# Two layers of attention and experts: shared sums by bank, token lists a step later, and an earlier turning of block 1

## The chip, the cores and the metric

The kernel runs on one core of a Trainium2 chip. Its time is the device time of one launch, in microseconds (us). The engines are TensorE (PE in the profile; its weight loads are PEld), VectorE (DVE), ScalarE (ACT), GpSimd (POOL) and SyncE (SP), which only issues transfers here. Each engine runs its own instructions in the order of the program, and waits on semaphores for the others.

## The reference

The input is 8 batches of 512 tokens with 256 channels, 4096 tokens in all. Four sublayers follow one another, each on the layer norm of what came before, each added to it. The change touches the second one, the first expert layer, in its shared part and in its routing.

```python
def _layernorm(x, axis=-1, eps=1e-05):
    m = jnp.mean(x, axis=axis, keepdims=True)
    v = jnp.var(x, axis=axis, keepdims=True)
    return (x - m) / jnp.sqrt(v + eps)

# x: (8, 512, 256), fp32. _L0_attn_ref is an attention without softmax (keys times values, then queries).
def _L0_ffn_ref(x, gate_w, wg, wu, wd, swg, swu, swd):     # 8 experts, top 2, INTER 352, 704 shared
    xf = x.reshape(-1, H)
    logits = xf.astype(jnp.float32) @ gate_w.astype(jnp.float32).T
    scores = jax.nn.softmax(logits, axis=-1)
    topw, topi = jax.lax.top_k(scores, TOP_K)
    denom = topw.sum(axis=-1, keepdims=True) + 1e-20
    topw = topw / denom * SCALE
    wdense = jnp.zeros((T, N_EXPERTS), jnp.float32).at[jnp.arange(T)[:, None], topi].set(topw)
    hg = jnp.einsum('th,ehi->eti', xf, wg)
    hu = jnp.einsum('th,ehi->eti', xf, wu)
    eo = jnp.einsum('eti,eih->eth', jax.nn.silu(hg) * hu, wd)
    y = jnp.einsum('te,eth->th', wdense, eo)
    shared = jax.nn.silu(xf @ swg) * (xf @ swu) @ swd
    return (y + shared).reshape(B, S, H)
...
    x = x + _L0_attn_ref(_layernorm(x, axis=-1), L0_attn_wq, L0_attn_wk, L0_attn_wv, L0_attn_wo)
    x = x + _L0_ffn_ref(_layernorm(x, axis=-1), L0_ffn_gate_w, L0_ffn_wg, L0_ffn_wu, L0_ffn_wd, L0_ffn_swg, L0_ffn_swu, L0_ffn_swd)
    x = x + _L1_attn_ref(_layernorm(x, axis=-1), ...)   # windowed softmax attention, 16 heads
    x = x + _L1_ffn_ref(_layernorm(x, axis=-1), ...)    # 8 experts, top 1, gelu, hidden 1024
    return x
```

## The kernel before, in words

A tile is 128 tokens; there are 32 of them, four to a batch. X holds the running sum of all tiles in SBUF. The program has four long parts.

**The mixture** (`pe_mix`, `dve_mix`, `act_mix`, 0 to 267 us of the trace). A loop of 46 steps mixes the first attention of all batches, the norm behind it, the gate's numbers, the shared expert of the first six batches and the routing. Every engine walks the same steps, each for itself; only semaphores tie them. The shared hidden layer of 704 is cut into six chunks, five of 128 and one of 64. For chunk n, numbered over the batches, the work is spread over three steps:

- the expansion on TensorE (`pe_shared_up`, L675, with 64 rows L667), in step n + 8. ScalarE takes SiLU of one half (`act_silu`, L1141), and VectorE multiplies it with the other (`dve_hidden`, L1434, "the product");
- the contraction on TensorE (`pe_shared_down`, L686), two steps later. It adds up in two PSUM banks, 0 and 1, each with two of the batch's four tiles. The six chunks of a batch accumulate there;
- after the sixth chunk VectorE adds both banks to X (`dve_shared_add`, L1444, "the sums"), in steps 15, 21, 27, 33, 39 and 45. The next batch's first contraction must find the banks empty. `fill` asks for this: it waits on the semaphore that `emptied` names for what the bank held, for the key "y" the counter s_added.

**The routing** runs on VectorE between this work, as a generator (`dve_find`) of which each step from 21 on takes a few calls at its end. 42 small instructions and three empty calls make the softmax, the two best experts, each token's slot in its expert's row of blocks, and each block's expert (L1557 is the last of them). Then come the lists, which invert this: a slot must say which token it holds. `dve_invert` makes 16 of them, one per call, each for four tiles and one of the two experts: four instructions, L1583, L1584, L1587 and L1588, of which the last tells TensorE. TensorE multiplies each list in four short bf16 matmuls (`pe_piece`, L711) and adds them up in one bank; two lists at the end of each of steps 34 to 41. Two empty calls follow, and then VectorE turns the bank into token numbers (L1597 to L1601). Lists have four buffers, so one waits until the fourth before it is read. How many calls a step takes stands in one line of `dve_mix`: four in the first steps, then two, and one in the step before the sums. It sets the order of VectorE's instructions.

**The first expert layer** (`pe_experts0` and its likes on the others, to about 574 us) works on 71 blocks of 128 slots. POOL gathers a block's token rows from DRAM (L1971, three buffers, so block b waits for the turning of block b - 3). TensorE turns them (`pe_turn_rows`, L768), block 0 in step 45 of the mixture already, and ScalarE copies the turned rows to SBUF (`act_turned_rows`, L1148). TensorE then computes the block's first products (`pe_up0`, L813, in bank b mod 2), which ScalarE and VectorE work up (L1157, L1756), then the rest (L823, L828) and the second products (L796). Behind the gather of block 4 POOL clears a buffer for the attention (L2008, the key pads).

**The second attention and the last expert layer** follow. The shared expert of the last two batches runs inside them, with the same functions and other banks.

Of the kernel before, what the change touches and what calls it, by code (L numbers as in the profile page):

```python
# [22 lines left out]
TPB = N // P  # L23
# [178 lines left out]
def build(nc, a, out):  # L202
    ctx = ExitStack()
    with ctx:
# [211 lines left out]
        def emptied(kind, *k):  # L416

            if kind == "turn":
                norm, b, c = k
                return (xnT_act, xnT_dve)[c], TURNED[norm, b] + 1  # L420
            if kind == "centre":
                return centred, 1
            if kind == "gate_out":
                return wo_made, 1
            if kind == "gate_proj":
                return wp_made, 1
            if kind == "kv":
                return kv_made, 2 * k[0] + k[1] + 1
            if kind == "q0":
                return q_made, k[0] + 1  # L430
            if kind == "energy":
                return en_made, k[0] + 1
            if kind == "fold":
                return ew_made, k[0] + 1
            if kind == "out":
                return a_added, TPB * k[0] + k[1] + 1
            if kind == "up":
                b, c, u = k
                return (sil_made, aTs_made)[u], b * NC + c + 1
            if kind == "y":  # L440
                return s_added, k[0] + 1
            if kind == "counts":
                return route_step, SLOTS_AT
            if kind == "invert":
                return tokens_made, 1
            if kind == "ranks":
                return counted, k[0] + 1
            if kind == "list":
                return tokens_listed, k[0] + 1
            if kind == "rows":  # L450
                l, b = k
                return xsT_made[l], b + 1
            if kind == "up0":
                return main_made, k[0] + 1
            if kind == "rest0":
                return aT0_made, min(2 * k[0] + 2, NBLK0)
            if kind == "down0":
                return y_made[0], k[0] + 1
            if kind == "scores":
                u, i, hd = k  # L460
                return mx_made, (u * TPB + i) * G + hd + 1
            if kind == "again":
                return p_exped, exps_before(*k) + 1
            if kind == "maxima":
                return maxima_placed, G // 2 * (k[0] + 1)
            if kind == "values":
                return oT_made, k[0] + 1
            if kind == "o":
                return o_made, k[0] + 1
            if kind == "qk":  # L470
                return lo_made, qk_number(*k) + 1
            if kind == "v":
                b, t = k
                return v_made, TPB * b + t + 1
            if kind == "project":
                b, c = k
                return (oT2_act, oT2_dve)[c], b + 1
            if kind == "residual":
                b, half, t = k
                return proj_added, TPB * b + 2 * half + t + 1  # L480
            if kind == "up1":
                return h_made, k[0] + 1
            if kind == "down1":
                return y_made[1], k[0] + 1
            raise KeyError(kind)

        def fill(e, key, bk):


            if bk in in_bank:  # L490
                e.wait_ge(*emptied(*in_bank[bk]))
            fills[bk] += 1
            in_bank[bk], bank_of[key], done[key] = key, bk, (bank_full[bk], fills[bk])
# [184 lines left out]

        def pe_shared_down(e, b, c, banks):
            w, q = SC[c], (b * NC + c) % 3  # L680
            if c == 0:
                for i, bk in enumerate(banks):
                    fill(e, ("y", b, i), bk)
            e.wait_ge(aTs_made, b * NC + c + 1)
            for t in range(TPB):
                m = e.matmul(psum[:, banks[t // 2], (t % 2) * E:(t % 2 + 1) * E], aT_s[0:w, q, t * P:(t + 1) * P], sdn[0:w, c, :],  # L686
                             start=(c == 0 and t % 2 == 0), stop=(c == NC - 1 and t % 2 == 1), skip_group_check=True)
                if c == NC - 1 and t % 2 == 1:
                    m.then_inc(bank_full[banks[t // 2]], 1)
                elif c < NC - 1 and t == TPB - 1:  # L690
                    m.then_inc(aTs_read, 1)
# [81 lines left out]
        def pe_experts0(e):  # L773
            o_ring = (6, 7)
            e.wait_ge(route_step, EXPERT_AT)
            e.wait_ge(wd0_loaded, 16 * 3)
            for s in range(NBLK0 + 5):
                b = s - 3
                if 0 <= b < NBLK0:
                    pe_up0(e, b)  # L780
                    if ends_pair(b):
                        pe_rest0(e, pair_of(b))
                b = s - 2
                if 0 < b < NBLK0:
                    pe_turn_rows(e, 0, b, xs0, next_of(T_RING))
                b = s - 5
                if b == NBLK0 - 1:

                    pe_shared_up(e, BM, 0, next_of(FIRST_RING), range(1))
                if b >= 0:  # L790
                    bk = next_of(o_ring)
                    fill(e, ("down0", b), bk)
                    e.wait_ge(aT0_made, b + 1)
                    x = e.value_load(blk_expert[0:1, 0, b:b + 1], min_val=0, max_val=NX - 1)
                    for c in range(DC):
                        m = e.matmul(psum[:, bk, 0:E], aT0[0:IC[c], b % 4, c * P:(c + 1) * P],  # L796
                                     wd0[0:IC[c], bass.ds(x, 1), c, :], start=(c == 0), stop=(c == DC - 1))
                    m.then_inc(bank_full[bk], 1)
# [564 lines left out]
        def dve_mix(e):  # L1363
# [3 lines left out]
            for s in range(MIX_STEPS):  # L1367
# [38 lines left out]
                if s >= ROUTED_AT:  # L1406

                    ends = any(c == NC - 1 for _, c in chunk(s, 1))
                    for _ in range(4 if s < ROUTED_AT + 12 else 1 if ends else 2):
                        next(finder, None)  # L1410
            for _ in finder:
                pass
# [24 lines left out]
        def dve_shared_add(e, b, banks):  # L1437

            t0 = b * TPB
            for i in range(2):  # L1440
                e.wait_ge(*done["y", b, i])
            for i in range(2):
                rows = X[:, t0 + 2 * i:t0 + 2 * i + 2, 0:E]
                m = e.tensor_tensor(rows, rows, psum[:, banks[i], :].rearrange("p (t c) -> p t c", t=2), ALU.add)  # L1444
            m.then_inc(s_added, 1)

        n_route = [0]

# [403 lines left out]
        def dve_add_fetched(e, t, j):  # L1852
            src, got, n = got_slot(t, j)
            if j == 0:
                e.wait_ge(s_added, t // TPB + 1)
            else:
                e.wait_ge(moe_added, 2 * t + 1)
            e.wait_ge(got, n)
# [387 lines left out]
```

## Time and profile before

| | us |
|---|---|
| median of 3 runs | 1386.27 |
| lowest and highest | 1384.47, 1387.79 |
| the profiled execution | 1384.07 |
| its span, first to last instruction | 1382.0 |
| TensorE busy | 1329.7 (96%) |
| VectorE busy | 687.0 (50%) |
| ScalarE busy | 488.3 (35%) |
| GpSimd busy | 446.8 (32%) |

The profile shows one execution. Its times count from the span's start. In a timeline a row is a run of equal instructions: start, length, engine, line of the kernel, destination and sources, how many, and in square brackets how long the engine stood idle ahead of it and which instruction released it. TensorE's lengths overlap a little, since matmuls are pipelined, and fp32 matmuls count several times; the distance from one start to the next is the surer measure of its pace. Idle time of an engine counts only where another one waits for its work.

### The profile page before, as it was taken

What the parts mean: (1) busy time and instruction counts of PE and PEld (TensorE: products, weight loads), DVE (VectorE), ACT (ScalarE), POOL (GpSimd) and SP (SyncE); (2) the same over time, 40 slices, a digit from 0 to 9 for tenths busy, and PEclk for the clock granted to TensorE, in tenths of its full rate; (3) what the DMA queues carried; (4) which work ended last, traced back from release to release, by engine and by line L of the source; (5) the groups of instructions that cost most, each with busy time, mean ns of one, the idle gap of its engine ahead of it and who ended that gap; (6) DMA issues with size and microseconds to landing.
All of it is one profiled execution on the core that took longest, in us unless ns stands there. A gap on an engine that the chain in (4) does not pass through costs nothing.

```text
span 1382.0 us, 25005 instructions
## 1 busy us (share of the span) xinstructions
PE 1329.7 (96%) x8348; PEld 1029.0 (74%) x8348; DVE 687.0 (50%) x2499; ACT 488.3 (35%) x1046; POOL 446.8 (32%) x541
## 2 busy tenths in 40 slices
PE   7899999999999999999999999999998999999998
PEld 5566556688999999755666666666665799999998
DVE  5655456233333333436888888888888231300000
ACT  2221211122222222122676676666766512111111
POOL 2100000253222222251554454544333534344332
PEclk9999999999999999999999999999999999999999
DMA  9402011067777777233555554655442789999996
GB/s 330 131 31 68 9 37 48 20 225 233 233 236 242 239 235 240 77 111 100 148 140 151 155 151 132 176 137 153 141 121 91 267 301 341 342 338 341 333 348 207
DMA packets 95676, 254.29 MB, mean 184 GB/s; under 512 B 12189, under 2 KB 42271, under 8 KB 85568
## 3 DMA queue, kind: packets, MB, share of 16 engines
q1 hardware_dynamic: 79728, 217.61, 48.5%
q0 software_dynamic: 12096, 32.13, 7.5%
q10 hardware_dynamic: 3728, 2.97, 0.7%
q8 instruction: 69, 1.13, 0.3%
q14 instruction: 55, 0.45, 0.1%
HBM read 201.42 MB, written 52.17 MB: 183 GB/s over the span
## 4 chain that ended last, share of the span: by engine, by line
PE 84%; DVE 8%; issue 4%; ACT 3%; DMA 0%; DVEq 0%; ACTq 0%; POOLq 0%
PE psum L994 10%; PE psum L675 10%; PE psum L1004 10%; PE psum L813 10%; PE psum L796 7%; PE psum L686 6%; PE psum L851 4%; PE psum L898 4%; PE psum L873 4%; PE psum L922 3%; DVE work L1892 3%; PE psum L823 2%; PE psum L768 2%; PE psum L933 2%; PE psum L956 2%
## 5 line engine op out<-in xcount | busy, mean ns | idle before, releaser
L1892 DVE CUSTOM_DVE_ANT_0 work<-psum,mask 128x384 bf16<-128x384 f32 (+1 forms) x512 | 230.0, 484 | 53.5 <-PE psum L851 52.2
L851 PE MATMUL psum<-kz,qT 96*128 96x384 f32 (+1 forms) x512 | 165.3, 391 | 14.2 <-DVE small L1892 12.9
L1971 POOL DMA_INDIRECT work<-normed,token_of x71 | 67.3, 948 | 323.6 <-PE psum L768 196.7
L675 PE MATMUL psum<-arena 128*128 128x512 f32 x320 | 147.5, 599 | 0.0
L994 PEld LDWEIGHTS psum<-arena 128*128 128x128 f32 x1248 | 145.5, 192 | 2.4 <-issue 0.4
L994 PE MATMUL psum<-arena 128*128 128x128 f32 x1248 | 146.1, 275 | 0.0
L813 PEld LDWEIGHTS psum<-work,arena 128*128 128x128 f32 x1136 | 134.9, 191 | 14.8 <-ACT work L1148 11.0
L813 PE MATMUL psum<-work,arena 128*128 128x128 f32 x1136 | 142.1, 278 | 3.6 <-ACT work L1148 2.0
L1244 ACT ACTIVATE arena<-psum 128x384 f32<-128x384 f32 x256 | 112.5, 496 | 85.4 <-PE psum L873 82.7
L1004 PE MATMUL psum<-arena 128*128 128x256 f32 x624 | 141.6, 379 | 0.8 <-issue 0.8
L873 PE MATMUL psum<-qT,kz 100*128 100x384 f32 (+1 forms) x512 | 131.9, 330 | 8.7 <-ACT arena L1244 8.4
L851 PEld LDWEIGHTS psum<-kz,qT 96*128 96x128 f32 x512 | 90.0, 192 | 64.6 <-DVE small L1892 37.5
L1746 DVE TENSOR_TENSOR arena<-psum,arena 128x256 f32<-128x256 f32 x39 | 16.6, 425 | 239.1 <-PE psum L1004 233.3
L1004 PEld LDWEIGHTS psum<-arena 128*128 128x128 f32 x624 | 115.4, 190 | 15.8 <-issue 1.8
L1272 ACT ACTIVATE arena<-psum 128x1024 f32<-128x1024 f32 x39 | 39.9, 1023 | 226.6 <-PE psum L994 203.3
L2037 POOL TENSOR_SCALAR_AFFINE_SELECT arena<-arena 128x512 f32<-128x512 f32 x96 | 62.3, 649 | 176.4 <-ACT arena L1244 152.1
L873 PEld LDWEIGHTS psum<-qT,kz 100*128 100x128 f32 x512 | 87.9, 189 | 30.0 <-ACT arena L1244 28.6
L796 PE MATMUL psum<-arena,work 128*128 (+1 forms) x426 | 103.8, 380 | 0.0
L675 PEld LDWEIGHTS psum<-arena 128*128 128x128 f32 x320 | 60.0, 192 | 57.9 <-issue 56.1
L1246 ACT ACTIVATE arena<-psum 128x512 f32<-128x512 f32 x128 | 75.4, 596 | 54.8 <-PE psum L873 49.0
L686 PE MATMUL psum<-arena,work 128*128 128x256 f32 (+1 forms) x384 | 91.9, 382 | 2.3 <-DVE X L1444 2.3
L686 PEld LDWEIGHTS psum<-arena,work 128*128 128x128 f32 (+1 forms) x384 | 71.3, 189 | 29.1 <-issue 17.6
(243 smaller groups left out, 1983.2 us busy)
## 6 DMA issues: line engine op xcount, KB each, us to landing
arena<-in_w SPq DMA_DIRECT2D x78, 1024.0 KB
arena<-in_wgu SPq DMA_DIRECT2D x71, 704.0 KB, 4.9
strips<-hi SPq DMA_DIRECT2D x64, 256.0 KB
kz<-strips SPq DMA_DIRECT2D x64, 192.0 KB, 3.2
qT<-strips SPq DMA_DIRECT2D x32, 384.0 KB, 4.7
results<-work SPq DMA_DIRECT2D x71, 128.0 KB
strips<-lo SPq DMA_DIRECT2D x32, 256.0 KB
normed<-work SPq DMA_DIRECT2D x14, 512.0 KB, 3.1
```

The source lines that it names most:

```text
L675: m = e.matmul(psum[0:w, bk, :], sgu[:, k, u, c * P:c * P + w], xnT_all[:, b, k, :], start=(k == 0), stop=(k == EC - 1))
L686: m = e.matmul(psum[:, banks[t // 2], (t % 2) * E:(t % 2 + 1) * E], aT_s[0:w, q, t * P:(t + 1) * P], sdn[0:w, c, :], start=(c == 0 and t % ...
L796: m = e.matmul(psum[:, bk, 0:E], aT0[0:IC[c], b % 4, c * P:(c + 1) * P], wd0[0:IC[c], bass.ds(x, 1), c, :], start=(c == 0), stop=(c == DC ...
L813: m = e.matmul(psum[:, b % 2, q * P:(q + 1) * P], wu0[:, b % 4, c, q * P:(q + 1) * P], xsT0[:, b % 2, c * P:(c + 1) * P], start=(c == 0), ...
L851: m = e.matmul(psum[:, bk, at:at + w], qT[0:ROWS_S, slot, half, i * P:(i + 1) * P], kz[slot][0:ROWS_S, hd, lo_key:hi_key], start=True, sto ...
L873: m = e.matmul(psum[:, bk, at:at + w], kz[slot][0:ROWS_T, hd, j * P:(j + 1) * P], qT[0:ROWS_T, slot, half, lo_q:hi_q], start=True, stop=True)
L994: m = e.matmul(psum[:, bk, q * P:(q + 1) * P], w1_now[k % 2][:, c, at:at + P], xsT1[:, k % 2, c * P:(c + 1) * P], start=(c == 0), stop=(c ...
L1004: m = e.matmul(psum[:, bk, 0:E], hT1[:, k % 2, c * P:(c + 1) * P], w2_now[k % 2][:, c, :], start=(c == 0), stop=(c == HC - 1))
L1244: e.activation(pT(u, j)[:, hd, 0:w], psum[:, bk, 0:w], ACT.Exp, scale=1.0 / E ** 0.5).then_inc(p_exped, 1)
L1246: e.activation(pT(u, j)[:, hd - 1:hd + 1, 0:w], psum[:, bk, :].rearrange("p (h n) -> p h n", h=2), ACT.Exp, scale=1.0 / E ** 0.5).then_inc ...
L1892: e.tensor_tensor_reduce(masked[:, n % 2, 0:w], psum[:, bank_of["scores", u, i, hd], at:at + w], mask[:, P - off:P - off + w], 1.0, MASKED ...
L1971: e.indirect_dma_start(out=xs[:, b % 3, :], out_offset=None, in_=normed[l][0:n, :], in_offset=bass.IndirectOffsetOnAxis(ap=token_of[:, l, ...
```

## The change

It has four edits.

1. The sums are signalled bank by bank: each of the two additions raises s_added, VectorE starts on bank 0 without waiting for bank 1, and all who wait on s_added count to twice the number. In the contraction of a batch's first chunk TensorE asks for bank 1 only before its third matmul.
2. In `dve_mix` the steps that take four calls of the routing end at step 31 instead of 32. Step 32, the one before the sums of step 33, takes one.
3. In `pe_experts0` block 1's rows are turned in front of block 0's products instead of behind them.
4. The last wait, of the routed sums for the shared ones, counts in the new way.

```diff
@@ -438,7 +438,7 @@
                 b, c, u = k
                 return (sil_made, aTs_made)[u], b * NC + c + 1
             if kind == "y":
-                return s_added, k[0] + 1
+                return s_added, 2 * k[0] + k[1] + 1
             if kind == "counts":
                 return route_step, SLOTS_AT
             if kind == "invert":
@@ -678,11 +678,10 @@
 
         def pe_shared_down(e, b, c, banks):
             w, q = SC[c], (b * NC + c) % 3
-            if c == 0:
-                for i, bk in enumerate(banks):
-                    fill(e, ("y", b, i), bk)
             e.wait_ge(aTs_made, b * NC + c + 1)
             for t in range(TPB):
+                if c == 0 and t % 2 == 0:
+                    fill(e, ("y", b, t // 2), banks[t // 2])
                 m = e.matmul(psum[:, banks[t // 2], (t % 2) * E:(t % 2 + 1) * E], aT_s[0:w, q, t * P:(t + 1) * P], sdn[0:w, c, :],
                              start=(c == 0 and t % 2 == 0), stop=(c == NC - 1 and t % 2 == 1), skip_group_check=True)
                 if c == NC - 1 and t % 2 == 1:
@@ -776,12 +775,14 @@
             e.wait_ge(wd0_loaded, 16 * 3)
             for s in range(NBLK0 + 5):
                 b = s - 3
+                if b == 0:
+                    pe_turn_rows(e, 0, 1, xs0, next_of(T_RING))
                 if 0 <= b < NBLK0:
                     pe_up0(e, b)
                     if ends_pair(b):
                         pe_rest0(e, pair_of(b))
                 b = s - 2
-                if 0 < b < NBLK0:
+                if 1 < b < NBLK0:
                     pe_turn_rows(e, 0, b, xs0, next_of(T_RING))
                 b = s - 5
                 if b == NBLK0 - 1:
@@ -1406,7 +1407,7 @@
                 if s >= ROUTED_AT:
 
                     ends = any(c == NC - 1 for _, c in chunk(s, 1))
-                    for _ in range(4 if s < ROUTED_AT + 12 else 1 if ends else 2):
+                    for _ in range(4 if s < ROUTED_AT + 11 else 1 if ends else 2):
                         next(finder, None)
             for _ in finder:
                 pass
@@ -1439,10 +1440,9 @@
             t0 = b * TPB
             for i in range(2):
                 e.wait_ge(*done["y", b, i])
-            for i in range(2):
                 rows = X[:, t0 + 2 * i:t0 + 2 * i + 2, 0:E]
-                m = e.tensor_tensor(rows, rows, psum[:, banks[i], :].rearrange("p (t c) -> p t c", t=2), ALU.add)
-            m.then_inc(s_added, 1)
+                e.tensor_tensor(rows, rows, psum[:, banks[i], :].rearrange("p (t c) -> p t c", t=2),
+                                ALU.add).then_inc(s_added, 1)
 
         n_route = [0]
 
@@ -1852,7 +1852,7 @@
         def dve_add_fetched(e, t, j):
             src, got, n = got_slot(t, j)
             if j == 0:
-                e.wait_ge(s_added, t // TPB + 1)
+                e.wait_ge(s_added, 2 * (t // TPB + 1))
             else:
                 e.wait_ge(moe_added, 2 * t + 1)
             e.wait_ge(got, n)
```

On VectorE, from the end of step 32 into step 33, the order before is the third list (list 2), then the sums, the product of step 33, and list 3:

```order
L1583 TENSOR_TENSOR work<-count,small 128x512
L1584 TENSOR_TENSOR work<-count,small 128x4x71
L1587 TENSOR_TENSOR work<-work,count 128x4x71
L1588 TENSOR_SCALAR work<-work,row_no 128x4x71
L1444 TENSOR_TENSOR X<-X,psum 128x2x256 x2
L1434 TENSOR_TENSOR work<-work,psum 128x512
L1583 TENSOR_TENSOR work<-count,small 128x512
```

and now, from the product of step 32 on:

```order
L1435 TENSOR_TENSOR work<-work,psum 128x512
L1557 TENSOR_SCALAR blk_expert<-work 128x71
L1444 TENSOR_TENSOR X<-X,psum 128x2x256 x2
L1435 TENSOR_TENSOR work<-work,psum 128x512
L1569 TENSOR_SCALAR small<-slot_of 128x32
L1570 TENSOR_SCALAR small<-slot_of 128x32
L1573 CAST small<-small 128x64
L1583 TENSOR_TENSOR work<-count,small 128x512
```

Three lists went from in front of the sums to behind them, and behind step 33's product. (Lines from the contraction on have moved by one: L1435 is the product, L685 the contraction, L767 the turning, L814 the first products.)

On VectorE where the routing ends, the order before is list 15, the products of steps 40 and 41, the token numbers, and the products of steps 42 and 43:

```order
L1583 TENSOR_TENSOR work<-count,small 128x512
L1584 TENSOR_TENSOR work<-count,small 128x4x71
L1587 TENSOR_TENSOR work<-work,count 128x4x71
L1588 TENSOR_SCALAR work<-work,row_no 128x4x71
L1434 TENSOR_TENSOR work<-work,psum 128x512 x2
L1597 COPY work<-psum 128x71
L1599 SCALAR_TENSOR_TENSOR work<-psum,work 128x71
L1601 CAST token_of<-work 128x71
L1434 TENSOR_TENSOR work<-work,psum 128x512
L1434 TENSOR_TENSOR work<-work,psum 64x512
```

and now, from the product of step 41 on:

```order
L1435 TENSOR_TENSOR work<-work,psum 128x512
L1583 TENSOR_TENSOR work<-count,small 128x512
L1584 TENSOR_TENSOR work<-count,small 128x4x71
L1587 TENSOR_TENSOR work<-work,count 128x4x71
L1588 TENSOR_SCALAR work<-work,row_no 128x4x71
L1435 TENSOR_TENSOR work<-work,psum 128x512
L1597 COPY work<-psum 128x71
L1599 SCALAR_TENSOR_TENSOR work<-psum,work 128x71
L1601 CAST token_of<-work 128x71
L1435 TENSOR_TENSOR work<-work,psum 64x512
```

List 15 stood two products ahead of the token numbers, in step 39; it now stands in step 41, behind the product of the step in which TensorE reads it. The token numbers stand behind the product of step 42 instead of 41.

On TensorE, from block 0's turning in step 45 over the last contraction into the first expert layer, the order before is:

```order
L768 MATMUL psum<-ident,work 128x128 x2
L686 MATMUL psum<-arena,work 128x256 x4
L813 MATMUL psum<-work,arena 128x128 x8
L768 MATMUL psum<-ident,work 128x128 x2
L813 MATMUL psum<-work,arena 128x128 x8
L823 MATMUL psum<-work,arena 128x128 x4
```

and now:

```order
L767 MATMUL psum<-ident,work 128x128 x2
L685 MATMUL psum<-arena,work 128x256 x4
L767 MATMUL psum<-ident,work 128x128 x2
L814 MATMUL psum<-work,arena 128x128 x16
L824 MATMUL psum<-work,arena 128x128 x4
```

The turning of block 1 stands between the contraction and block 0's products, which block 1's follow at once.

## Rows read from the trace of the kernel before

**Rows 1.** The page: chain that ended last, share of the span

```profile
PE 84%; DVE 8%; issue 4%; ACT 3%; DMA 0%; DVEq 0%; ACTq 0%; POOLq 0%
```

**Rows 2.** Stretches (us): length, busy us and counts, TensorE clock, DMA share, GB/s

```profile
190.00:270.00 80.00, 76.15 (x296) 47.53 (x295) 44.23 (x102) 8.70 (x15) 4.02 (x4) 1.00 0.12 43
...
300.00:560.00 260.00, 259.58 (x1989) 234.55 (x1988) 82.71 (x217) 73.43 (x220) 62.34 (x64) 1.00 0.73 235
```

**Rows 3.** Line of the shared sums: who waited for it, us and times

```profile
  PE psum L686: 2.3, 1
  PE psum L813: 1.5, 1
```

**Rows 4.** Timeline, TensorE, 202 to 210 us: start, length, engine, line; idle before

```profile
202.04 3.70 PE L675 MATMUL psum<-arena 128*128 128x512 f32 x8
208.05 1.97 PE L686 MATMUL psum<-arena,work 128*128 128x256 f32 x8 [2.31 <-DVE X L1444]
```

**Rows 5.** Timeline, VectorE, 200 to 208 us

```profile
200.93 0.19 DVE L1557 TENSOR_SCALAR blk_expert<-work 128x71 int32<-128x71 f32 x1
...
201.68 0.69 DVE L1583 TENSOR_TENSOR work<-count,small 128x512 bf16<-128x512 f32 x1
...
206.67 1.28 DVE L1444 TENSOR_TENSOR X<-X,psum 128x512 f32<-128x512 f32 x2
```

**Rows 6.** Timeline, TensorE, 236 to 248 us

```profile
236.14 1.99 PE L686 MATMUL psum<-arena,work 64*128 64x256 f32 x8
238.06 3.70 PE L675 MATMUL psum<-arena 128*128 128x512 f32 x8
241.60 0.92 PE L711 MATMUL psum<-work 128*128 128x213 bf16 x8
242.35 1.91 PE L686 MATMUL psum<-arena,work 128*128 128x256 f32 x8
...
247.53 0.92 PE L711 MATMUL psum<-work 128*128 128x213 bf16 x8
```

**Rows 7.** Timeline, VectorE, 241 to 245 us

```profile
241.90 0.69 DVE L1434 TENSOR_TENSOR work<-work,psum 128x512 f32<-128x512 f32 x1 [0.83 <-PE psum L675]
242.50 0.69 DVE L1583 TENSOR_TENSOR work<-count,small 128x512 bf16<-128x512 f32 x1
...
243.96 0.29 DVE L1588 TENSOR_SCALAR work<-work,row_no 128x284 bf16<-128x284 bf16 x1
244.17 0.68 DVE L1583 TENSOR_TENSOR work<-count,small 128x512 bf16<-128x512 f32 x1
```

**Rows 8.** Timeline, VectorE, 253 to 256 us

```profile
253.76 0.69 DVE L1434 TENSOR_TENSOR work<-work,psum 128x512 f32<-128x512 f32 x1 [5.25 <-PE psum L675]
...
254.95 0.20 DVE L1601 CAST token_of<-work 128x71 int32<-128x71 f32 x1
```

**Rows 9.** Timeline, POOL, 255 to 274 us

```profile
255.45 1.18 POOL L1971 DMA_INDIRECT work<-normed,token_of  x1 [124.56 <-DVE token_of L1601]
...
270.92 0.94 POOL L1971 DMA_INDIRECT work<-normed,token_of  x1 [4.76 <-PE psum L768]
273.68 1.80 POOL L2008 MEMSET kz<- 96x2048 f32 x1 [1.81 <-DMA work<-normed,token_of]
```

**Rows 10.** Timeline, TensorE, 264 to 272 us

```profile
264.56 0.38 PE L768 MATMUL psum<-ident,work 128*128 128x128 f32 x2
264.88 1.99 PE L686 MATMUL psum<-arena,work 64*128 64x256 f32 x8
268.41 2.02 PE L813 MATMUL psum<-work,arena 128*128 128x128 f32 x16 [1.54 <-DVE X L1444]
270.26 0.38 PE L768 MATMUL psum<-ident,work 128*128 128x128 f32 x2
271.18 1.05 PE L813 MATMUL psum<-work,arena 128*128 128x128 f32 x7 [0.53 <-ACT work L1148]
```

**Rows 11.** Timeline, ScalarE, 270 to 272 us

```profile
270.46 0.38 ACT L1157 ACTIVATE work<-psum 128x256 f32<-128x256 f32 x1 [5.10 <-PE psum L813]
270.75 0.38 ACT L1148 ACTIVATE work<-psum 128x256 f32<-128x256 f32 x1
```

## Prediction

> **What bounds the kernel now.** I began with the page's chain that ended last: 84% of it is TensorE [rows 1]. The table of stretches then shows the first expert layer, 300 to 560 us, at 259.58 us of TensorE work in 260, and the end of the mixture, 190 to 270 us, at 76.15 in 80, all at a granted clock of 1.00, so 2.4 GHz [rows 2]. So whatever TensorE loses or gains before 300 us moves all that follows by as much: there is no slack behind it that could swallow it. Third, the line of the shared sums: TensorE waited for it in two places that count, 2.3 and 1.5 us [rows 3]. The timelines around these two places, and around the places to which the change moves work, give the rest. I call an execution of the mixture's loop body a step; the product's row on VectorE (SiLU times up) tells where a step stands.
>
> **Place 1, the pause at 205.6 us (gone).** In step 32 VectorE finishes the routing and then makes three lists, 201.68 to 206.7, ahead of step 33's sums, which start at 206.67 and end at 207.95 [rows 5]. TensorE's contraction of step 34 needs both sum banks. Its expansion before began at 202.04, and from such a start to the next group is 3.54 (238.06 to 241.60 [rows 6]), so it could have gone at 205.58; it went at 208.05 [rows 4]. Loss 2.47. In the changed order VectorE has only the routing's last instruction there (ends 201.12 [rows 5]); the banks are full when the next group starts, 202.04 [rows 4], both sums (206.67 to 207.95, 1.28) end by about 203.4, 2.2 us before TensorE wants them. Saved: **-2.47**. Bank by bank adds nothing here, since both sums are early by more than one bank's 0.69.
>
> **Place 2, the lists (new waits).** Lists are numbered 0 to 15; TensorE multiplies two of them at the end of each of steps 34 to 41 (eight short matmuls). Before, VectorE made 14 and 15 in step 39 and was well ahead. Now 45 calls stand before list 0, of which 44 fall in steps 21 to 31 and one in 32; so list 0 and 1 come in step 33, 2 and 3 in 34, 4 and 5 in 35, 6 and 7 in 36, 8 and 9 in 37, **only 10 in 38** (the step before a sum gives one), 11 and 12 in 39, 13 and 14 in 40, 15 in 41. TensorE wants 10 and 11 at the end of step 39, 12 and 13 in 40, 14 and 15 in 41. So 11, 13 and 15 are made in the very step that reads them. And there each is queued behind that step's product, which waits for that step's expansion on TensorE, the work right before the lists' matmuls. VectorE cannot be early: the wait is built in. A list also waits until the fourth before it is read (8, made in 37, for 4, read in 36); that binds nowhere now.
>
> Its size, from the same pattern in step 39 of before: TensorE's list matmuls began at 241.60 [rows 6]; the product began at 241.90, the list behind it at 242.50, its last instruction at 243.96 for 0.29, so 244.25 [rows 7]. From the semaphore to TensorE some 0.1 (sums end 207.95, TensorE starts 208.05 [rows 4, 5]). So the second list can begin 0.30 + 0.60 + 1.75 + 0.1 = 2.75 after the first. Unhindered it begins at half of the group's 0.75 (241.60 to 242.35 [rows 6]), 0.38. Each pause 2.37. After a pause TensorE's whole next step moves along with it, and the product too, so the second and third are as long. **+7.11** for three. Bounds: below, 3 x (0.60 + 1.75 - 0.38) = 5.9, if the product starts with the lists' matmuls; above, 3 x 2.75 = 8.3, if the first list's matmuls hide nothing.
>
> The earlier lists are in time. From step to step is 5.93 (241.60 to 247.53 [rows 6]); the second list of a step is ready 0.30 + 0.60 + 1.67 + 1.75 = 4.3 after the expansion's end, the 1.67 being the distance 242.50 to 244.17 [rows 7]. The tightest is step 37, whose expansion has 64 rows and half of the matmuls: 5.93 - 1.77 = 4.16, plus 0.38 for list 7, so 4.54 against 4.3. Step 33 has three short conversions more, 0.5 us, against 5.2. If these slip it is by 0.2 each.
>
> **Place 3, token numbers a step later.** Before, they were made behind the product of 253.76, the last instruction at 254.95 for 0.20 [rows 8], the gather issued at 255.45 [rows 9]: 1.69 after the product. Now they stand behind the next product, 5.93 later, so in before's time the gather goes at 261.38. TensorE turns block 0 at 264.56 [rows 10]. How long a gather takes to land is seen once: issued 270.92 for 0.94, and POOL, which waited for it, went on at 273.68, 2.76 later [rows 9]. The first gather's issue is 0.24 longer (1.18), so 3.0: landed at 264.4, 0.2 before its use. Block 1 follows about 1.5 us behind, so 265.9, and is used at 266.8. I take **0**, with bounds 0 and +1.2 (4.2 to land, if transfers compete; in this stretch the DMA share is 0.12 [rows 2]). The Trainium skill ("DMA: Bandwidth & Descriptors", Anatomy of one DMA) gives a fixed part of about 2.0 us, mostly the write's receipt, plus bytes over 436 GB/s. By it the estimate for 128 KB would be 2.3 us, 0.5 short of the 2.76 that the row shows from issue to use; the row decides.
>
> **Place 4, the first expert blocks.** The last contraction of the mixture begins at 264.88; at its usual pace (236.14 to 238.06, the same shape, 1.92 [rows 6]) it is through at 266.80. The first block's products need bank 0, and began at 268.41 [rows 10] behind both sums. Now one sum is enough, and bank 0 is full half way, at about 265.9; its sum takes 0.69, so 266.7. Block 1's turning now stands in front, 266.80 to 267.12, inside what was pause. First block at 267.12: **-1.29**. The turning's move itself earns nothing. ScalarE keeps its order: SiLU of block 0 (270.46), and only then the copy of block 1's turned rows (270.75 to 271.13), after which TensorE starts block 1 at 271.18 [rows 10, 11]. So from block 0's start to block 1's stays 2.77, with the turning out of it and 0.9 of pause in place of 0.5. The queue behind on POOL: the gather of block 4 waits for block 1's turning and goes some 3 us earlier relative to the blocks, and the key pads behind it too; from 300 to 560 TensorE waits for nothing [rows 2], so 0. Bounds of this place: -1.6 and -0.6 (if the bank counts as full only with the whole group, half of the gain goes).
>
> **Rest.** The extra wait inside a contraction, one a batch, finds its bank free; the sums' extra increments cost no instruction. 0, bounds -0.1 to +0.3.
>
> Sum: -2.47 + 7.11 + 0 - 1.29 = **+3.35 us**. On the profiled execution, 1384.07 with its span of 1382.0, that is 1387.4. The median of the runs is 2.20 above the profiled one, so I add to the median: 1386.27 + 3.35 = **1389.6**.
>
> **Rivals.**
> *A, faster: the late lists cost nothing.* Then the two savings stand alone, 1386.27 - 3.76 = 1382.5. It needs list 11 to be ready when TensorE comes, thus the product of step 39 to be done before the expansion's end. For it: VectorE has time, it stood idle for 0.83 before the product of 241.90. Against it: that idle time is the wait for TensorE itself [rows 7]. The point from which it decides is the total pause at the three places: below 3.8 us the change wins. 0.08.
> *B, rows late.* Block 0's gather takes 4.2 rather than 3.0, TensorE stands at its turning for 1 to 1.2: 1390.8. For it: only 0.2 of margin. Against: DMA is nearly idle there. 0.09.
> *C, clock.* Three pauses within 18 us and the granted clock falls to the lower level, 1.2 GHz. The stretch with the 2.3 us pause kept 1.00 [rows 2]. If each pause made the following 5.9 us run at half speed, it would be +17.7 more: 1407. The Trainium skill ("TensorE: Matmul & The Clock Gate", Why this matters for your kernels) says that idle gaps between bursts of matmuls throw the clock back to the lower level; the one gap of this kind in the trace did not. 0.03.
> *D, evened out.* The pauses are there, but shorter by the bounds above, or something later gives a part back: +0 to +2.5, say 1387.5. For it: the attention's VectorE, not TensorE, may bound parts behind 560. Against: the chain passes on a later start. 0.12.
> *Forecast*, 1387.9 to 1391.5 with what a median of three wanders: 0.68.
>
> **Numbers.** A measurement of this kernel can tell about 0.2%, 2.8 us. The forecast lies only 0.6 above that, so I count 0.50 of its 0.68 as slower and 0.18 as same. With B and C slower, D two thirds same and one third slower, A faster: slower 0.64, same 0.27, faster 0.09. The range leaves out C and most of A: 1385.0 to 1392.2.
>
> **What would show it.** In the profile after: no wait for the sums at the contraction of step 34; three waits of TensorE's list matmuls for VectorE's last list instruction, 2.2 to 2.5 each, 8.3 us apart; token numbers 10.6 us later by the clock (5.93 + 7.11 - 2.47); block 0's turning without a wait above 0.3; block 0's products right behind the turning of block 1; then 0.9 before block 1; from block 1 on every row later by 3.35. Wrong would be: fewer than three such waits, waits of under 1.5, or a wait for the gather of over 0.5.

## The result, and the profile after

| | before | changed |
|---|---|---|
| median, same chip, 11 runs each (us) | 1384.47 | 1388.63 |
| lowest, highest | 1382.52, 1387.79 | 1386.04, 1390.96 |
| profiled execution, its span | 1384.07, 1382.0 | 1389.49, 1387.5 |

The ratio of the times is 1.003, with a 95% interval of 1.0019 to 1.0041. The change makes the kernel 4.2 us slower (2.6 to 5.7); 3.35 were forecast. A second pair gave 1.0036 (1.0022 to 1.005). Where a kernel below had executions in a slower state (one list late: 1728 and 3385 us), its median leaves them out.

The first place to look is the list of TensorE's waits from 195 to 300 us, longest in total first (line, whom it waited for, us in total, times, longest). Of the changed kernel:

```profile
PE psum L710 <- DVE work L1588: 6.5, 3, 2.2
PE psum L814 <- ACT work L1149: 1.8, 2, 1.1
```

L710 are the lists' matmuls, L1588 the last instruction of a list on VectorE. The two waits for the sums [rows 3] are gone, and three waits for lists stand in their place. The timeline of TensorE at step 34 shows what went:

```profile
202.10 3.70 PE L675 MATMUL psum<-arena 128*128 128x512 f32 x8
205.64 1.89 PE L685 MATMUL psum<-arena,work 128*128 128x256 f32 x8
```

3.54 from one start to the next, as in an undisturbed step, where before it was 6.01 [rows 4]. And the timeline from step 39 on shows what came:

```profile
239.11 0.54 PE L710 MATMUL psum<-work 128*128 128x213 bf16 x4
241.82 0.55 PE L710 MATMUL psum<-work 128*128 128x213 bf16 x4 [2.17 <-DVE work L1588]
242.21 1.91 PE L685 MATMUL psum<-arena,work 128*128 128x256 f32 x8
243.95 3.60 PE L675 MATMUL psum<-arena 128*128 128x512 f32 x8
247.39 0.54 PE L710 MATMUL psum<-work 128*128 128x213 bf16 x4
250.09 0.55 PE L710 MATMUL psum<-work 128*128 128x213 bf16 x4 [2.17 <-DVE work L1588]
250.48 3.59 PE L685 MATMUL psum<-arena,work 128*128 128x256 f32 x8
253.87 3.63 PE L675 MATMUL psum<-arena 128*128 128x512 f32 x8
257.34 0.54 PE L710 MATMUL psum<-work 128*128 128x213 bf16 x4
260.05 0.55 PE L710 MATMUL psum<-work 128*128 128x213 bf16 x4 [2.17 <-DVE work L1588]
260.44 3.33 PE L685 MATMUL psum<-arena,work 128*128 128x256 f32 x8
263.56 3.90 PE L675 MATMUL psum<-arena 128*128 128x512 f32 x8
267.30 1.89 PE L685 MATMUL psum<-arena,work 128*128 128x256 f32 x8
```

The eight matmuls of two lists are torn into four and four, with 2.17 between. From their start to the contraction's is 3.10 (239.11 to 242.21), against 0.75 [rows 6]: 2.35 a pause, 7.05 for three. VectorE's side of the second pause shows the order that does it:

```profile
247.68 0.69 DVE L1435 TENSOR_TENSOR work<-work,psum 128x512 f32<-128x512 f32 x1 [4.26 <-PE psum L675]
248.29 0.68 DVE L1583 TENSOR_TENSOR work<-count,small 128x512 bf16<-128x512 f32 x1
...
249.74 0.29 DVE L1588 TENSOR_SCALAR work<-work,row_no 128x284 bf16<-128x284 bf16 x1
```

VectorE had stood idle for 4.26, but behind a product that waits for TensorE.

There is a second loss in that timeline. The contractions at 250.48 and 260.44 take 3.39 and 3.12 to the next start instead of 1.74 (242.21 to 243.95), with nothing they wait for. The table of stretches (length, busy us and counts of the engines, TensorE's granted clock, DMA share, GB/s) names it:

```profile
240.00:250.00 10.00, 6.10 (x24) 3.64 (x24) 5.64 (x15) 0.60 (x1) 0.00 (x0) 1.00 0.00 0
250.00:260.00 10.00, 7.79 (x24) 4.82 (x24) 3.98 (x10) 0.60 (x1) 0.00 (x0) 0.83 0.01 2
260.00:270.00 10.00, 9.95 (x31) 6.51 (x32) 1.26 (x4) 0.60 (x1) 0.77 (x1) 0.83 0.00 0
```

In shorter cuts, 250.50 to 253.90 us has a granted clock of 0.50 and 260.40 to 263.60 one of 0.56: behind the second and the third pause TensorE ran at 1.2 GHz instead of 2.4 for a while. With the expansions behind them this cost 3.39 + 3.47 + 3.12 + 3.74 - 2 x (1.74 + 3.43) = 3.4 us.

At the first expert blocks the changed kernel's TensorE shows:

```profile
272.47 0.38 PE L767 MATMUL psum<-ident,work 128*128 128x128 f32 x2
272.79 1.99 PE L685 MATMUL psum<-arena,work 64*128 64x256 f32 x8
274.71 0.44 PE L767 MATMUL psum<-ident,work 128*128 128x128 f32 x2
274.98 1.95 PE L814 MATMUL psum<-work,arena 128*128 128x128 f32 x16
...
277.68 2.05 PE L814 MATMUL psum<-work,arena 128*128 128x128 f32 x16 [0.75 <-ACT work L1149]
```

From the last contraction's start to block 0's products is 2.19 (before 3.53), and to block 1's 4.89 (before 6.30 [rows 10]): 1.41 saved. So up to block 1 the sum is -2.47 + 7.05 - 1.41 = +3.17 without the low clock and +6.5 with it. Block 1 starts at 277.68 against 271.18: +6.50. The span grew by 5.5, the later parts of this execution being 1.0 shorter in all, although they hold a low stretch that the profile before doesn't have (1040 to 1060 us at 0.91).

### The profile page after: what moved, and what is told of

The parts are those of the page before. It is cut to its first block, busy times and chain, and to the rows that moved or that the text cites. A ratio compares the mean times of both kernels' runs of the same rounds, so it can differ in the third digit from the quotient of the medians.

```text
span 1387.5 us, 24998 instructions
## 1 busy us (share of the span) xinstructions
PE 1333.7 (96%) x8348; PEld 1032.6 (74%) x8348; DVE 687.7 (50%) x2499; ACT 489.0 (35%) x1046; POOL 447.3 (32%) x541
## 4 chain that ended last, share of the span: by engine, by line
PE 84%; DVE 8%; issue 4%; ACT 3%; DMA 0%; DVEq 0%; ACTq 0%; POOLq 0%
PE psum L675 10%; PE psum L995 10%; PE psum L1005 10%; PE psum L814 9%; PE psum L797 7%; PE psum L685 6%; PE psum L899 4%; PE psum L852 4%; PE psum L874 4%; PE psum L923 3%; DVE work L1892 2%; PE psum L824 2%; PE psum L767 2%; PE psum L934 2%; ACT arena L1245 2%
## 5 line engine op out<-in xcount | busy, mean ns | idle before, releaser
L814 PEld LDWEIGHTS psum<-work,arena 128*128 128x128 f32 x1136 | 134.9, 191 | 12.4 <-ACT work L1149 10.6
L814 PE MATMUL psum<-work,arena 128*128 128x128 f32 x1136 | 142.0, 278 | 1.8 <-ACT work L1149 1.8
L685 PE MATMUL psum<-arena,work 128*128 128x256 f32 (+1 forms) x384 | 95.0, 391 | 0.0
L1142 ACT ACTIVATE work<-psum 128x512 f32<-128x512 f32 (+1 forms) x48 | 28.6, 596 | 184.9 <-PE psum L675 147.6
```

The costliest lines, as they stand in the source:

```text
L814: m = e.matmul(psum[:, b % 2, q * P:(q + 1) * P], wu0[:, b % 4, c, q * P:(q + 1) * P], xsT0[:, b % 2, c * P:(c + 1) * P], start=(c == 0), ...
```

## The experiments

"Local sum" is what the distances between TensorE's starts show up to block 1, against 6.01, 0.75 and 6.30 of before, without the low clock. "Clock loss" is an estimate from the mean granted clock and the span of every execution: the average of (1 - mean clock) x span, which is what an execution loses if TensorE has work throughout, less the same of before. A clock is given to 0.001, 1.4 us of one execution, so only the averages say something, to about 1 us. Times in us; each ratio is to the kernel before on the same chip (on one of them, with 1389.72, it is slower throughout, and its mean clocks are lower).

| kernel | median, before's beside it | ratio (95%) | difference | local sum | clock loss |
|---|---|---|---|---|---|
| changed | 1388.63, 1384.47 | 1.003 (1.0019 to 1.0041) | +4.2 | +3.2 | no clocks of before |
| changed, again | 1388.58, 1383.68 | 1.0036 (1.0022 to 1.005) | +4.9 | +3.2 | +1.5 |
| edit 2 undone | 1379.84, 1384.58 | 0.996 (0.9945 to 0.9976) | -4.7 | -2.0 | -3.5 |
| edit 2 alone | 1396.01, 1389.72 | 1.005 (1.0036 to 1.0064) | +6.3 | +4.6 | +0.1 |
| three lists in step 33 | 1378.25, 1384.58 | 0.995 (0.9936 to 0.9964) | -6.3 | -3.9 | -2.6 |
| the same, again | 1378.86, 1383.68 | 0.9962 (0.9948 to 0.9976) | -4.8 | -3.9 | -1.3 |
| one list late | 1381.17, 1384.58 | 0.9972 (0.9961 to 0.9982) | -3.4 | -1.5 | -1.9 |
| two lists late | 1384.78, 1384.58 | 0.9998 (0.9987 to 1.0009) | +0.2 | +0.8 | -1.6 |
| pauses filled | 1389.84, 1389.72 | 1.0003 (0.9992 to 1.0014) | +0.1 | +3.2 | -3.4 |
| three in 33, turning behind | 1383.81, 1389.72 | 0.9959 (0.9946 to 0.9973) | -5.9 | -4.0 | -2.7 |
| three in 33, sums together | 1386.41, 1389.72 | 0.9977 (0.9967 to 0.9987) | -3.3 | -2.5 | -2.6 |
| three in 33, copy ahead | 1375.96, 1383.68 | 0.9949 (0.9936 to 0.9963) | -7.7 | -4.9, to block 2 | -2.4 |
| before, again | 1383.55, 1383.68 | 1.0 (0.9991 to 1.0009) | -0.1 | 0 | -0.1 |

**Edit 2 undone.**

```diff
-                    for _ in range(4 if s < ROUTED_AT + 11 else 1 if ends else 2):
+                    for _ in range(4 if s < ROUTED_AT + 12 else 1 if ends else 2):
```

> The changed kernel with edit 2 undone: step 32 takes four calls again, so lists 0 to 2 stand ahead of the sums of step 33. Theory (late lists cost it all): no pause of TensorE at its list matmuls; the pause at step 34's contraction is back, but bank by bank it is one sum shorter, 0.6 to 0.7 us; the first expert block starts 1.3 early. So 1.9 us faster than before, about 1382.6 against 1384.5. Granted clock 1.00 from 200 to 300 us. Rival (the loss comes from the sums by bank or from the turning in front): it stays 3 to 4 us slower than before.

Faster by 4.7, so the loss is edit 2's. The pause at step 34 is back, one sum shorter:

```profile
PE psum L814 <- ACT work L1149: 1.8, 2, 1.1
PE psum L685 <- DVE X L1444: 1.8, 1, 1.8
```

The size was missed: 4.7 where 1.9 was expected, and the interval leaves 1.9 out. This opened the question of the low clock in the kernel before, below.

**Edit 2 alone**, the same line the other way round in the kernel before.

> The kernel before with edit 2 alone: the calls of step 32 put off, nothing else. Theory: the pause at step 34 goes (-2.47), three pauses of 2.35 come (+7.05), and one or two stretches at the lower clock (0 to +3.3): 4.6 to 7.9 slower than before, 1389 to 1392.4 against 1384.5; the first expert block gains nothing. Rival (edit 2 is harmless and the loss is of another edit): level with before or 2.5 faster.

Slower by 6.3, with the same three waits. Its profile has low stretches behind the first and the third pause, and one behind the 1.5 us wait for the sums.

**Three lists in step 33.**

```diff
-                    for _ in range(4 if s < ROUTED_AT + 11 else 1 if ends else 2):
+                    for _ in range(4 if s < ROUTED_AT + 11 else 1 if ends else 2 + (s in (33,))):
```

> The changed kernel with one call more in step 33, so that three lists are made there and from step 34 on every list stands where it stood before the change. Theory: no list is late, both savings stay, 2.47 + 1.34 = 3.8 us faster than before, about 1380.7; no stretch at the lower clock between 200 and 300 us. Rival (token numbers made a step later hold up block 0): TensorE waits 1 us or more at block 0's turning, gain under 2.8.

Of TensorE's waits from 195 to 300 us this is left:

```profile
PE psum L814 <- ACT work L1149: 1.8, 2, 1.1
```

One call more, in the right step, keeps what edit 2 was worth and takes all three pauses away: TensorE waits for no list, at block 0's turning it doesn't wait, though the token numbers are made in step 42 as in the changed kernel, and the clock is 1.00 from 200 to 300 us. More was gained than the 3.8 expected.

**One list late, and two.** The same line with (39,) and with (40,).

> The changed kernel with one call more in step 39: list 11 is late as before, 13 and 15 are not. One pause of 2.35 us instead of three. Theory (2.35 us a pause, and the clock falls only where pauses repeat): 3.8 - 2.35 = 1.5 us faster than before, 1383.0, clock 1.00 throughout 240 to 270 us. Rival (any such pause drops the clock): a stretch at 0.50 follows, and it is 0.2 slower to level with before.

> The changed kernel with one call more in step 40: lists 11 and 13 are late, 15 is not. Two pauses, 4.7 us. Theory: 4.7 - 3.8 = 0.9 slower than before by the pauses, and up to 1.7 more for one stretch at the lower clock behind the second pause, which is where the changed kernel's profile has its first: 1385.4 to 1387.1. Rival (the low clock needs three pauses): 1.00 throughout, 1385.4.

Medians on one chip go 1378.25, 1381.17, 1384.78 for none, one and two pauses: 2.9 and 3.6 a pause, of which 2.35 are the wait. With one pause the profile keeps 1.00; with two it shows one low stretch, behind the second:

```profile
250.00:260.00 10.00, 10.00 (x37) 6.84 (x38) 3.85 (x9) 0.60 (x1) 0.00 (x0) 0.83 0.01 2
```

**Pauses filled.**

```diff
             bk = bank_of["invert",]
             last = TOP[0] * NT // CH - 1
+            if n in (11, 13, 15):
+                e.wait_ge(route_step, SLOTS_AT)
+                for _ in range(9):
+                    e.matmul(psum[:, bank_of["counts",], 0:P], ones[:, :], before[:, :], start=True, stop=True)
             e.wait_ge(pieces_made, n + 1)
```

> The changed kernel with nine needless fp32 matmuls of 128 columns (about 2 us) on TensorE ahead of its wait for lists 11, 13 and 15, into a bank that is free by then. The waits end no sooner, but TensorE is not idle in them. Theory (the low clock comes from idling): granted clock 1.00 from 240 to 270 us, TensorE's waits for those lists down to 0.1 to 0.5, and the time 3.3 us better than the changed kernel's in runs with both stretches, 0 to 3.3 on the median; 1385.5 to 1388.5 against 1388.6. Rival (the slow contractions behind the pauses come from something else, as a port shared with VectorE): they stay slow, 630 ns a matmul, and the time is as the changed kernel's or longer.

The needless matmuls (fp32, so each counts twice) go where the pause was, and the next contraction starts as late as in the changed kernel (237.55 to 240.65 is 3.10, the same). But it runs at full speed:

```profile
237.55 0.54 PE L714 MATMUL psum<-work 128*128 128x213 bf16 x4
237.93 2.19 PE L711 MATMUL psum<-before,ones 128*128 128x128 f32 x18
240.26 0.55 PE L714 MATMUL psum<-work 128*128 128x213 bf16 x4
...
248.92 1.91 PE L685 MATMUL psum<-arena,work 128*128 128x256 f32 x8
250.67 3.60 PE L675 MATMUL psum<-arena 128*128 128x512 f32 x8
```

Its stretches of 10 us from 240 to 270 are at 1.00. VectorE's work is the same, so the slow contractions were not contention with it: they come from TensorE standing idle. That is one profile, but all executions on this chip say the same: their mean clock is 0.994 on average, against 0.992 of edit 2 alone and of before. The kernel with useless work in it is level with before, where the changed one, which didn't run beside it, is 1.003 and 1.0036. Edit 2 alone, which did, is 6.2 slower than the filled one; 1.4 of that are local. Its median misses the expected range of 1385.5 to 1388.5, but that was reckoned for a chip on which before needs 1384.5, and here it needs 1389.7.

**Turning behind.** As three in step 33, with the turning of block 1 behind block 0's products.

```diff
-                if b == 0:
-                    pe_turn_rows(e, 0, 1, xs0, next_of(T_RING))
...
-                if 1 < b < NBLK0:
+                if 0 < b < NBLK0:
```

> As the kernel with three lists in step 33, but block 1's rows are turned behind block 0's products again. Theory (the turning's move earns nothing): block 0's products start 0.3 earlier, or as soon as the first sum is there, the turning then fills part of the pause before block 1, and block 1 starts within 0.2 of where it does with the turning in front: level with the kernel with three lists in step 33, about 1380.7. Rival (the move is worth something): 0.3 us or more slower from block 1 on.

```profile
263.31 1.99 PE L685 MATMUL psum<-arena,work 64*128 64x256 f32 x8
265.31 2.02 PE L812 MATMUL psum<-work,arena 128*128 128x128 f32 x16
...
268.08 2.05 PE L812 MATMUL psum<-work,arena 128*128 128x128 f32 x16 [0.53 <-ACT work L1147]
```

From the last contraction's start to block 1's products it is 4.77 (263.31 to 268.08), against 4.90 with the turning in front (264.00 to 268.90). The move earns nothing; it costs 0.13, since the turning delays block 0 and the pause behind it was there anyway. The whole time can't tell 0.13: 5.9 under before here, 6.3 and 4.8 for three lists in step 33 on two other chips.

**Sums together.** As three in step 33, with one increment behind both sums, and the waits counted as before.

```diff
-                return s_added, 2 * k[0] + k[1] + 1
+                return s_added, k[0] + 1
...
             for i in range(2):
                 e.wait_ge(*done["y", b, i])
+            for i in range(2):
                 rows = X[:, t0 + 2 * i:t0 + 2 * i + 2, 0:E]
-                e.tensor_tensor(rows, rows, psum[:, banks[i], :].rearrange("p (t c) -> p t c", t=2),
-                                ALU.add).then_inc(s_added, 1)
+                m = e.tensor_tensor(rows, rows, psum[:, banks[i], :].rearrange("p (t c) -> p t c", t=2), ALU.add)
+            m.then_inc(s_added, 1)
...
```

> As the kernel with three lists in step 33, but the sums are signalled once, after both banks. Theory: block 0's products wait for both sums again, which start only when both banks are full; block 0 starts 1.2 to 1.3 later relative to the contraction, nothing changes at step 34: 2.5 us faster than before, 1382.0. Rival (the bank-wise signal also matters at step 34): the pause at step 34 comes back in part.

```profile
264.42 2.02 PE L814 MATMUL psum<-work,arena 128*128 128x128 f32 x16 [1.17 <-DVE X L1445]
```

Contraction to block 1 is 6.30 again (260.89 to 267.19), with a wait of 1.17 for the sums before block 0, and nothing comes back at step 34. So all of place 4's gain is the sums', 1.4 us. On one chip it is 2.6 slower than the kernel with the turning behind; 1.5 are local.

**Before, again.** The kernel before, unchanged, to see where the surplus comes from.

> The kernel before, unchanged, for a second profile and the mean clock of each run. Open: the kernel with three lists in step 33 gained 6.3 us, and what its trace shows saved between 200 and 280 us is 3.8. Theory (the pauses of before, 2.3 and 1.5 us, are in some runs followed by a stretch at the lower clock, 1.7 us lost each): its runs have mean clocks that vary by 0.001 to 0.003, the longer the lower, and the profile may show a stretch at 0.50 behind 208 or 268 us. Rival (the surplus is in the later parts and has nothing to do with the pauses): mean clocks all alike, times as much apart as before.

Its second profile is as the first up to the wait for the sums, and then:

```profile
264.75 1.99 PE L686 MATMUL psum<-arena,work 64*128 64x256 f32 x8
268.28 3.62 PE L813 MATMUL psum<-work,arena 128*128 128x128 f32 x16 [1.54 <-DVE X L1444]
271.74 0.38 PE L768 MATMUL psum<-ident,work 128*128 128x128 f32 x2
```

Block 0's products take 3.46 to the next start, where they took 1.85 [rows 10], and the stretch shows why:

```profile
268.00:272.00 4.00, 3.72 (x18) 3.63 (x18) 0.13 (x1) 0.07 (x1) 0.00 (x0) 0.57 0.00 0
```

So the kernel before, too, loses 1.6 us behind its pause in one of two profiles. Over its 26 runs on this chip the mean clock and the time go together roughly: 1382.4 to 1383.5 at 0.995, 1383.1 to 1385.6 at 0.994, 1384.4 and 1384.7 at 0.992, and 1387.4 at 0.991; 0.993 has both 1385.4 and 1387.3.

**Changed, again, and three in step 33, again.**

> The changed kernel, unchanged, beside the one before on the same chip. Theory: 3.3 us plus what the low clock takes, so 3 to 6 us slower; three pauses of 2.2; zero to three stretches at 0.50 behind them. Rival: within 2 us of before.

> The kernel with three lists in step 33 a second time. Theory: block 1's first products start 3.8 earlier than in the second profile of before, or more by 1.7 for each stretch at 0.50 that this one shows between 200 and 280; the rest of the time's difference lies behind 560 us. Rival (its 6.3 of before was scatter): 3.8 or less on the whole time.

The changed kernel has its three waits and two low stretches in the same places. The other has none from 200 to 300 us; its block 1 starts at 269.25, against 272.65 in before's second profile, though its expansion ahead of step 34 came 2.14 later (204.06, against 201.92). Corrected for that the distance is 5.5, the local 3.9 and the 1.6 of before's low stretch.

**Copy ahead.** As three in step 33, with ScalarE's copy of block 1's turned rows ahead of its SiLU of block 0.

```diff
                 b = s - 2
-                if 0 <= b < NBLK0:
+                if b == 0:
+                    act_turned_rows(e, 0, 0, xsT0)
+                    act_turned_rows(e, 0, 1, xsT0)
+                if 1 < b < NBLK0:
                     act_turned_rows(e, 0, b, xsT0)
```

> As the kernel with three lists in step 33, and ScalarE copies block 1's turned rows ahead of block 0's SiLU instead of behind it. Theory (the turning in front earns nothing only because ScalarE's order was left as it was): block 1's products follow block 0's without a wait, 1.75 to 1.9 after them instead of 2.70, so 0.8 to 0.9 faster than the kernel with three lists in step 33. Rival (block 2 or bank 1's sum is then late and takes it back): TensorE's wait before block 2 grows from 1.1 to about 2.

Block 1 follows without a wait, and block 2's wait stays what it was:

```profile
262.29 1.99 PE L685 MATMUL psum<-arena,work 64*128 64x256 f32 x8
264.21 0.44 PE L767 MATMUL psum<-ident,work 128*128 128x128 f32 x2
264.48 3.74 PE L814 MATMUL psum<-work,arena 128*128 128x128 f32 x32
...
271.15 1.05 PE L814 MATMUL psum<-work,arena 128*128 128x128 f32 x7 [1.08 <-ACT work L1149]
```

ScalarE copies block 1's rows at 264.68 now, beside block 0's products. To block 2 it is 8.86 (262.29 to 271.15), against 9.88 in the kernel with three in step 33. It is the fastest of all: 1375.96, 7.7 us under before and 12.6 under the changed kernel on the same chip. It is also 2.9 under three lists in step 33 there, where 0.8 to 0.9 were expected; 1.0 is local, by the estimate of the table 1.1 is the clock, and the rest is within what medians of five wander.

## Why the prediction was right

- **Place 1**, -2.47: measured 6.01 - 3.54 = 2.47.
- **Place 2**, +7.11: three pauses of 2.35, 7.05, each in the step and at the list that counting the calls had given. That the gain at one end of this edit is paid back threefold at the other could be read from the order of instructions and one undisturbed step of the trace. The kernels with none, one, two and three late lists rise in this order.
- **Place 3**, 0: TensorE's turning of block 0 came 3.24 after the gather's issue (269.23 to 272.47) without a wait. Rival B is out. How large the margin was no row shows; 0.2 rests on the estimate of 3.0 for a landing.
- **Place 4**, -1.29: measured -1.41, all of it from the sums by bank. That the turning's move earns nothing was right, and why was, too: with ScalarE's order turned as well it is worth 0.9 to 1.0.
- **Rest**, 0: no wait shows it.
- **Rival A**, that late lists cost nothing, fell with 6.5 us of waits.
- **Rival D**, evened out: each pause was 2.35 where 2.37 was worked out, and the median's difference lies above the sum, not below it.
- **Rival C**, the clock, got 0.03 and a price of 17.7. That was wrong in both: the granted clock did fall in both profiles of the changed kernel, behind two pauses of three, and it cost 1.7 a time, 3.4 in all. I had taken it that one pause without a drop, in one execution, speaks against drops. It spoke for one execution, and that same trace has the low clock elsewhere, behind an idle time of 3.75 us that ended at 41.66, and behind idle times of 1.38, 0.69 and 0.60 from 640 us on:

```profile
40.00:60.00 20.00, 18.34 (x80) 11.40 (x81) 12.73 (x44) 5.13 (x12) 2.01 (x2) 0.91 0.61 180
640.00:660.00 20.00, 16.50 (x68) 11.81 (x68) 15.93 (x68) 9.66 (x17) 6.20 (x7) 0.83 0.51 134
```

The stretches read for the prediction [rows 2] left both out. They would have given a drop a real chance, and a price: 0.09 of 20 us is 1.8 for the first of them, where 5.9 was assumed for each pause. The Trainium skill ("TensorE: Matmul & The Clock Gate", Why this matters for your kernels), which has idle gaps set the clock back, has the cause right: filling the gaps kept the clock.

- The measured 4.2 and 4.9 stand 1.0 and 1.7 above the local sum. The clock gives the sign and most of the size. By the table the changed kernel, again, loses 1.5 more to the clock than before, where its difference is 1.7 above its local sum, and the nine rows with a negative clock loss of over 1 us lose 1.3 to 3.5 less, where their differences are 0.6 to 3.1 below theirs. The two agree within about 1 us, except for the kernel with the sums together (1.8 apart) and edit 2 alone (1.6 apart). The number of pauses alone doesn't give the loss: two lists late has two, as before has, and loses 1.6 less. Not all of it lies at these pauses: the profiles have low stretches at 640 to 660 us in every kernel, and at 40 to 60, 660 to 700 and 1020 to 1060 us in some. How often each pause brings the drop was not counted, so the split by pause stays open.
- The time, 1389.6, was met within 1.0 by luck in part: before's median of eleven is 1.8 below the median of three it started from, and the difference came out 0.8 larger. The mechanism stands on the waits, not on this.
- Of the signs named beforehand three failed, all by the low clock: token numbers came 13.8 us later by the clock (gather at 269.23, against 255.45) and not 10.6, block 1 came 6.50 later and not 3.35, and the third wait ended 9.96 behind the second and not 8.3. The waits were 2.17, just under the 2.2 to 2.5 named.
- The chances in the prediction's last sum don't add up as stated: its own terms give slower 0.66, same 0.26, faster 0.08. Nothing hangs on it.

## What to carry to other kernels

When work is put off so that something else is early, count forward to the step where its last piece is read, not only the place where it was in the way: here one call less in a loop pushed three pieces behind an instruction that waits for their own reader. One call more, one step later, had both. And an instruction moved forward earns only what the next engine's order lets it: turn that order as well, or leave it. Before a clock drop is ruled out, read the granted clock over the whole trace, and of more than one execution.

## What the runs showed of the hardware

TensorE's granted clock can fall to half behind idle times of 1.5 to 2.2 us, in some executions of a kernel and not in others (behind before's idle time of 1.54 in one profile of two; behind the first of three of 2.17 in one profile of three). The matmuls behind it then lose 1.6 to 1.7 us, 1.3 in one case (edit 2 alone, behind 1.54), so that a pause of 2.35 cost 2.9 and 3.6 on the median. Nine needless matmuls in the pause (2.2 us of work) kept the clock at 1.00 in the one profile taken, though the wait lasts as long.
